# Gates of a mixture of experts: broadcast by TensorE against broadcast by DMA from a DRAM scratch

## The chip, the cores and the metric

One core of one Trainium2 chip runs the whole program. The metric is the device time of one execution in microseconds; lower is better. Below, batch b is one of four sequences (0 to 3) and a pair is one or two tiles of 128 hidden units of the experts.

## The reference, cut to what matters

The layer adds a selective scan over a context to `x`, and then a feed-forward layer of 2 shared and 32 routed experts, of which each token takes 6. All arrays are fp32: `x` is (4, 256, 256), the context (4, 256, 128), each expert's hidden size is 176.

```python
x = x + ssm(ctx, layernorm(x))              # scan over 256 steps, 256 channels x 16 states
xf = layernorm(x)                           # tokens x 256
shared = sum(relu(xf @ sw1[e] + sb1[e]) @ sw2[e] + sb2[e] for e in range(2)) / 2
logits = xf @ router_w + router_b
p, i = top_k(softmax(logits), 6); p = p / p.sum(-1)
gates = zeros(tokens, 32).at[rows, i].add(p)
routed = sum(gates[:, e:e+1] * (relu(xf @ rw1[e] + rb1[e]) @ rw2[e] + rb2[e]) for e in range(32))
out = x + shared + routed
```

## The kernel before

Everything lies transposed: features or hidden units on the 128 partitions, the 256 tokens of a batch on the free axis. The hidden units of all experts are laid end to end: 3 tiles of 128 for the shared ones, 44 for the routed ones (32 x 176 = 44 x 128, so most tiles hold units of two experts). They are worked in 24 pairs of tiles, `PAIRS`; pair 0 has the shared tiles 0 and 1, pair 1 only tile 2, and pairs 2 to 23 are routed.

A pair goes through the engines like this. TensorE makes the first layer into PSUM tile `z` with three fp32r products for each of two halves of the features (high and low parts of weights and input, L474 to L476), 12 matmuls. ScalarE adds the bias and takes the relu into `hg` (L613). TensorE has meanwhile made `gb`, the gates spread over the partitions: one matmul for each tile of a constant 0/1 matrix `selg` with `gst`, the 32 gates of the 256 tokens as three bf16 parts stacked on 96 partitions (L483). VectorE multiplies `hg` by `gb` (L796; pairs 0 and 1 are scaled by 1/2 at L798 instead). Three pairs later (`SKEW`) TensorE adds the second layer into `acc` (`second_layer`, L455): 4 fp32 matmuls, which the trace shows as 8 pieces, in batches 0 to 2, and 12 fp32r matmuls in the last batch, where ScalarE, GpSimd and VectorE make high and low parts (`split`). The trace calls `hg` by the tile it is a view of, `stage`, and drops digits from names, so `w` is `w2` or `w1` and `x` is `x1`.

Beside the pairs of batch b run the steps of the scan and router of the next batches, at pairs that tables name (`UNITS`, `ZGATE`, `BACK`, `NEXT`): in pairs 0 to 15 one unit of the scan each (`bu`, scan and product with C on VectorE, decay on ScalarE, the spread of B in even pairs and of C in odd ones on TensorE, L368 and L377, a fold on GpSimd), `stats` in pair 2, `zmul` in pair 10, and after pair 16 the norm, the router's logits and `gates`. The order on each engine is fixed by the program; engines wait for each other by semaphores. The run begins with a head (0 to 91 us) in which the first batch's scan has no expert work beside it. Batch 0 is opened by the lists in `OPEN`.

The gates of a batch are made in `gates` (L772) on VectorE, split into three bf16 parts (L786 to L789), turned by TensorE in pair 1 (`turn`, L429), and copied by ScalarE into `gst` and `gT` (L623, L624). `gT`, the fp32 form, is needed for the second layer's bias in pair 4. PSUM is full: `z` 2 banks, `gb` 2, `acc`, `bb`, `cc`, `misc` one each. So the first layer of pair p waits for the product of pair p - 2, the last reader's turn of both double buffers:

```python
if exists(b, p, 2):
    pe.wait_ge(S["hg_done"], b * NP + p - 1)
```

SyncE issues every DMA. In the expert phase that is one load of second-layer weights a pair, into a ring of six (`load_w2`), as soon as the second layer that frees the slot is done (`next_w2`), one store of the output and one load of the next `x1` a batch.

## Time and profile before

| what | value |
| --- | --- |
| time, median of 3 runs (range) | 433.68 us (433.26 to 436.71) |
| the profiled execution's own time | 433.63 us |
| its span, first to last instruction | 431.6 us |
| mean granted TensorE clock | 0.952 of full |
| busy: PE, DVE, ACT, POOL | 91%, 72%, 50%, 28% |
| the chain's share: PE, DVE, issue, ACT | 80%, 12%, 6%, 1% |
| DMA busy share, all of it in queue 1 (SyncE's) | 28.8% |

The chain is the sequence of work that ended last, followed back from the final instruction; an engine's share of it, and not its busy share, says how much of the time hangs on that engine. TensorE's rows overlap: one that is listed as 0.28 us long is followed by the next after 0.12, so differences between starts are what counts.

### The profile page before, as it was taken

How to read it: one execution, taken by the hardware profiler on the slowest of the kernel's cores; microseconds unless marked ns; L12 is line 12 of the kernel's file. 1: busy time of each engine (PE TensorE's matmuls, PEld its weight loads, DVE VectorE, ACT ScalarE, POOL GpSimd, SP SyncE). 2: the span in 40 equal slices, each digit the busy share in tenths (PEclk: the TensorE clock that was granted, in tenths of full speed). 3: DMA queues.
4: the chain of work that ended last, by engine and by line, in shares of the span. 5: the costliest groups of instructions: out<-in, count | busy, mean ns of one | idle time of the engine just before them, and what ended most of it. 6: DMA issues, size and time to landing. Idle time of an engine off the chain costs nothing.

```text
span 431.6 us, 7326 instructions
## 1 busy us (share of the span) xinstructions
PE 392.4 (91%) x2559; PEld 350.5 (81%) x2559; DVE 310.2 (72%) x544; ACT 215.9 (50%) x482; POOL 119.5 (28%) x88
## 2 busy tenths in 40 slices
PE   5565588589999999999999999999999999999996
PEld 3343366478899999978999989889999999999996
DVE  3499997799798767898898568898984544344443
ACT  3777625446443434565443436565432345556562
POOL 0654432013233200033333000233331023344432
PEclk8659889669999999999999999999999999999999
DMA  7344473002222322331222212332222224233320
GB/s 225 104 137 110 136 199 144 2 25 74 73 75 57 90 52 60 95 101 50 74 71 73 73 49 69 105 90 69 75 73 74 74 61 123 73 80 93 83 65 26
DMA packets 18879, 36.49 MB, mean 85 GB/s; under 512 B 2082, under 2 KB 4932, under 8 KB 18756
## 3 DMA queue, kind: packets, MB, share of 16 engines
q1 hardware_dynamic: 18852, 36.13, 28.8%
q8 instruction: 16, 0.26, 0.2%
q14 instruction: 11, 0.09, 0.1%
HBM read 35.08 MB, written 1.05 MB: 84 GB/s over the span
## 4 chain that ended last, share of the span: by engine, by line
PE 80%; DVE 12%; issue 6%; ACT 1%; DVEq 0%; ACTq 0%
PE acc L455 34%; PE z L474 10%; PE z L476 9%; PE z L475 9%; PE gb L483 4%; DVE bu L702 3%; PE z L387 2%; DVE bu L695 2%; PE acc L353 2%; PE bb L368 1%; PE cc L377 1%; PE acc L460 1%; PE bb L395 1%; PE misc L414 1%; PE cc L402 1%
## 5 line engine op out<-in xcount | busy, mean ns | idle before, releaser
L613 ACT ACTIVATE stage<-z,par 128x256 f32<-128x256 f32 x188 | 79.0, 471 | 159.6 <-PE z L476 159.5
L455 PE MATMUL acc<-stage,w 128*128 128x256 f32 x564 | 134.6, 381 | 0.0
L474 PE MATMUL z<-xh,w1l 128*128 128x256 f32 (+1 forms) x376 | 120.5, 321 | 0.0
L455 PEld LDWEIGHTS acc<-stage,w 128*128 128x128 f32 x564 | 102.6, 191 | 12.3
L796 DVE TENSOR_TENSOR stage<-stage,gb 128x512 f32<-128x512 f32 x88 | 60.3, 686 | 70.5 <-ACT stage L613 69.6
L846 POOL TENSOR_TENSOR ya<-ya,pr 128x512 f32<-128x512 f32 x42 | 54.8, 1305 | 196.7 <-DVE pr L713 196.7
L475 PE MATMUL z<-xl,w1h 128*128 128x256 f32 (+1 forms) x376 | 106.7, 284 | 0.0
L476 PE MATMUL z<-xh,w1h 128*128 128x256 f32 (+1 forms) x376 | 106.7, 284 | 0.0
L702 DVE TENSOR_TENSOR_SCAN bu<-dA,bu 128x512 f32<-128x512 f32 x64 | 78.6, 1237 | 2.0 <-ACT dA L566 0.4
L474 PEld LDWEIGHTS z<-xh,w1l 128*128 128x128 f32 x376 | 71.9, 191 | 4.0 <-issue 2.2
L475 PEld LDWEIGHTS z<-xl,w1h 128*128 128x128 f32 x376 | 72.1, 192 | 1.7
L476 PEld LDWEIGHTS z<-xh,w1h 128*128 128x128 f32 x376 | 72.0, 191 | 0.0
L566 ACT ACTIVATE dA<-delta,aneg 128x255 f32<-128x255 f32 x128 | 57.4, 502 | 16.3 <-DVE bu L702 15.5
L863 POOL TENSOR_TENSOR w2l<-w,w2h 128x512 fp32r<-128x512 f32 (+1 forms) x24 | 31.8, 1324 | 68.7 <-ACT w2h L620 68.7
L695 DVE TENSOR_TENSOR bu<-bb,du 128x512 f32<-128x512 f32 x64 | 43.1, 683 | 1.3 <-PE bb L368 1.3
L713 DVE TENSOR_TENSOR pr<-bu,cc 128x512 f32<-128x512 f32 x50 | 33.9, 685 | 12.2 <-PE cc L377 8.7
L830 POOL TENSOR_TENSOR w1l<-stage,w1h 128x1024 fp32r<-128x1024 f32 (+1 forms) x12 | 28.6, 2382 | 40.3 <-ACT w1h L511 23.6
L483 PE MATMUL gb<-gst,selg 96*128 96x256 bf16 x176 | 35.2, 282 | 0.0
L455 PE MATMUL acc<-hh,w2l 128*128 128x256 f32 x94 | 28.0, 298 | 0.0
L455 PE MATMUL acc<-hl,w2h 128*128 128x256 f32 x94 | 26.3, 280 | 0.0
L455 PE MATMUL acc<-hh,w2h 128*128 128x256 f32 x94 | 26.2, 279 | 0.0
L377 PE MATMUL cc<-bcs,selbc 96*128 96x256 bf16 x64 | 13.7, 300 | 11.3 <-DVE pr L713 7.8
(122 smaller groups left out, 408.2 us busy)
## 6 DMA issues: line engine op xcount, KB each, us to landing
w<-in_w SPq DMA_DIRECT2D x92, 256.0 KB, 2.7
stage<-in_w SPq DMA_DIRECT2D x11, 512.0 KB, 3.6
selg<-in_selg SPq DMA_DIRECT2D x1, 1056.0 KB, 7.7
x<-in_xT SPq DMA_DIRECT2D x4, 256.0 KB, 3.9
out<-x SPq DMA_DIRECT2D x4, 256.0 KB, 2.6
xr<-in_xr SPq DMA_DIRECT2D x1, 768.0 KB, 9.8
w<-in_w SPq DMA_DIRECT2D x4, 128.0 KB, 2.0
par<-in_par SPq DMA_DIRECT2D x1, 385.5 KB
```

The lines of the kernel that those rows point to most:

```text
L455: mm = pe.matmul(acc[:, k, :], weights, h, start=t + k + n == 0, stop=last, skip_group_check=True)
L474: pe.matmul(z[p % 2][:, i, :], w1l[:, t, one], xh_, start=k == 0, stop=False)
L475: pe.matmul(z[p % 2][:, i, :], w1h[:, t, one], xl_, start=False, stop=False)
L476: mm = pe.matmul(z[p % 2][:, i, :], w1h[:, t, one], xh_, start=False, stop=k == KD - 1)
L483: mm = pe.matmul(gb[p % 2][:, i, :], selg[:, t - NT_S, :], gst[:], start=True, stop=True)
L566: ins = act.activation(dA[:, k, j * L + 1:(j + 1) * L], delta[:, k, 1:L], ACT.Exp, scale=aneg[:, n:n + 1])
L613: ins = act.activation(hg[:, p % 4, i, :], z[p % 2][:, i, :], ACT.Relu, bias=b1[:, t:t + 1])
L695: dve.tensor_tensor(bu[:, k, :].rearrange("p (j l) -> p j l", j=2), bb[:], du[:, k:k + 1, :].broadcast_to([P, 2, L]), ALU.mult).then_inc(S ...
L702: dve.tensor_tensor_scan(bu[:, k, :], dA[:, k, :], bu[:, k, :], 0.0, ALU.mult, ALU.add).then_inc(S["scan_done"], 1)
L713: dve.tensor_tensor(products(b, c)[:, k, :], bu[:, k, :], cc[:].rearrange("p a b -> p (a b)"), ALU.mult).then_inc(S["prod_done"], 1)
L796: ins = dve.tensor_tensor(hg[:, p % 4], hg[:, p % 4], gb[p % 2][:], ALU.mult)
L846: pool.tensor_tensor(ya[:, k, :], ya[:, k, :], pr[:, k, :], ALU.add).then_inc(S["y_folded"], 1)
```

## The change

The gate no longer goes through TensorE. Four things change together.

1. The experts are tiled anew. The first 128 hidden units of each of the 32 experts make one tile each (pairs 2 to 17, `NSINGLE` = 16), so one gate holds for a whole tile; the remaining 48 units of each, end to end, make 12 tiles (pairs 18 to 23).
2. `gT` is stored to a DRAM scratch, `gates`, and read back with a partition step of 0: one DMA for each of the 16 single pairs (`gate_one`, 256 KB into the ring `gone` of four), and 40 DMAs of 16 to 48 rows for the remainder (`gate_rem`, 1.5 MB into `grem`), four in each of pairs 4 to 13. SyncE issues all of them, 57 more in a batch.
3. ScalarE writes the relu back into its PSUM bank, and VectorE makes the product from PSUM and the gate in SBUF into `hg`. `gb`'s two banks go to `z`, which has four, so the first layer of pair p waits for the product of pair p - 4.
4. The turn has no bf16 part, VectorE's bf16 split goes, and the turn moves from pair 1 to the end of pair 23 of the batch before (batch 0: pair 0), so that the gates leave early.

To make room, `xr` and `ctxT` are kept for two batches and loaded as the run goes, and `hh` and `hl` have three buffers in place of four.

```diff
@@ tables and buffers
-TURN_AT = 1
+ZB = 4
+GRING = 4
...
-        ("xh", 21), ("xl", 21), ("top", 21), ("ex", 22), ("gates", 22)]
+        ("xh", 21), ("xl", 21), ("top", 21), ("ex", 22), ("gates", 22), ("turn", 23)]
...
-BEHIND = ("mean", "logits", "xall", "dt")
+BEHIND = ("mean", "logits", "xall", "dt", "turn")
...
-OPEN = [[("gates", 0)],
+OPEN = [[("gates", 0), ("turn", 0)],
...
-        z = [ps(f"z{i}", [P, 2, L]) for i in range(2)]
-        gb = [ps(f"gb{i}", [P, 2, L]) for i in range(2)]
+        z = [ps(f"z{i}", [P, 2, L]) for i in range(ZB)]
@@ SyncE
+            def gate_one(b, p):
+                e = 2 * (p - SINGLE0)
+                eng.dma_start(gone[:, p % GRING], gates_d[b % 2, e:e + 2, :].rearrange("(o e) l -> o e l", o=1).broadcast_to(
+                    [P, 2, L])).then_inc(ld_g[p % GRING], 16)
+
+            def gate_rem(b, part):
+                for e, t, at, n in SEGMENTS[part::REMPARTS]:
+                    eng.dma_start(grem[at:at + n, t, :], gates_d[b % 2, e:e + 1, :].broadcast_to([n, L])).then_inc(ld_rem, 16)
...
+            for b in range(B):
+                eng.wait_ge(S["gates_done"], b + 1)
+                eng.dma_start(gates_d[b % 2], gT[0:NR, :]).then_inc(S["spilled"], 16)
+                if b:
+                    eng.wait_ge(S["hg_done"], b * NP)
+                eng.wait_ge(S["spilled"], 16 * b + 16)
+                for p in range(SINGLE0, SINGLE0 + GRING):
+                    gate_one(b, p)
                 for p in range(NP):
...
+                    if SINGLE0 <= p < SINGLE0 + NSINGLE - GRING:
+                        eng.wait_ge(S["hg_done"], b * NP + p + 1)
+                        gate_one(b, p + GRING)
+                    if 4 <= p < 4 + REMPARTS:
+                        gate_rem(b, p - 4)
...
+                    if p >= SKEW:
+                        if b < B - 1 or p - SKEW < NP - RING:
+                            next_w2(b, p - SKEW)
+                    elif b:
+                        next_w2(b - 1, p - SKEW + NP)
@@ TensorE
+                elif name == "turn":
+                    pe.wait_ge(S["g34_done"], b + 1)
+                    for t in range(2):
+                        mm = pe.matmul(misc[0:NR + NSH, 1, t * P:(t + 1) * P], g34[:, t, :], ident, start=True, stop=True)
+                    mm.then_inc(S["turned"], 1)
...
-                if exists(b, p, 2):
-                    pe.wait_ge(S["hg_done"], b * NP + p - 1)
+                if exists(b, p, ZB):
+                    pe.wait_ge(S["hg_done"], b * NP + p - ZB + 1)
...
-                if PAIRS[p][0] >= NT_S:
-                    if PAIRS[p][0] == NT_S:
-                        pe.wait_ge(ld_selg, 16)
-                        pe.wait_ge(S["gates_done"], b + 1)
-                    for i, t in enumerate(PAIRS[p]):
-                        mm = pe.matmul(gb[p % 2][:, i, :], selg[:, t - NT_S, :], gst[:], start=True, stop=True)
-                    mm.then_inc(S["gb_ready"], 1)
-                if p == TURN_AT:
-                    turn(b)
@@ ScalarE
-                    ins = act.activation(hg[:, p % 4, i, :], z[p % 2][:, i, :], ACT.Relu, bias=b1[:, t:t + 1])
+                    ins = act.activation(z[p % ZB][:, i, :], z[p % ZB][:, i, :], ACT.Relu, bias=b1[:, t:t + 1])
...
-                if p == TURN_AT:
-                    act.wait_ge(S["turned"], b + 1)
-                    act.activation(gst[:], miscb[0:3 * NR, 0:L], ACT.Copy)
-                    act.activation(gT[:], misc[0:NR + NSH, 1, :], ACT.Copy).then_inc(S["gates_done"], 1)
@@ VectorE
-                    own.then(dve.tensor_copy(g3[:, :, 0, :], g34[:, :, 0:NR]))
-                    own.then(dve.tensor_tensor(gr[:], g34[:, :, 0:NR], g3[:, :, 0, :], ALU.subtract))
-                    own.then(dve.tensor_copy(g3[:, :, 1, :], gr[:]))
-                    dve.tensor_tensor(g3[:, :, 2, :], gr[:], g3[:, :, 1, :], ALU.subtract).then_inc(S["g3_done"], 1)
...
-                if PAIRS[p][0] >= NT_S:
-                    dve.wait_ge(S["gb_ready"], b * NPR + p - (NP - NPR) + 1)
-                    ins = dve.tensor_tensor(hg[:, p % 4], hg[:, p % 4], gb[p % 2][:], ALU.mult)
+                if p >= SINGLE0 + NSINGLE:
+                    r = 2 * (p - SINGLE0 - NSINGLE)
+                    dve.wait_ge(ld_rem, (b + 1) * 16 * len(SEGMENTS))
+                    ins = dve.tensor_tensor(hg[:, p % 4], z[p % ZB][:], grem[:, r:r + 2, :], ALU.mult)
+                elif p >= SINGLE0:
+                    dve.wait_ge(ld_g[p % GRING], b * (16 * NSINGLE // GRING) + 16 * ((p - SINGLE0) // GRING + 1))
+                    ins = dve.tensor_tensor(hg[:, p % 4], z[p % ZB][:], gone[:, p % GRING], ALU.mult)
```

TensorE, an even pair of the loop's body. Before:

```order
L476 MATMUL z<-xh,w1h 128x256
L483 MATMUL gb<-gst,selg 128x256 x2
L361 ISA
L368 MATMUL bb<-bcs,selbc 128x256 [waits bu_done]
L368 MATMUL bb<-bcs,selbc 128x256
L455 MATMUL acc<-stage,w 128x256 [waits ld_w2_3,hg_done]
L455 MATMUL acc<-stage,w 128x256 x3
```

After:

```order
L512 MATMUL z<-xh,w1h 128x256
L399 ISA
L406 MATMUL bb<-bcs,selbc 128x256 [waits bu_done]
L406 MATMUL bb<-bcs,selbc 128x256
L477 REGISTER_ALU
L491 MATMUL acc<-stage,w 128x256 [waits ld_w2_3,hg_done]
L491 MATMUL acc<-stage,w 128x256 x3
```

The two `gb` matmuls between the first layer and the scan's B are gone; the rest keeps its place, and what the first layer waits for is two pairs older.

TensorE at the turn of the gates. Before, it stands between the first layer of pair 1 and its second layer:

```order
L476 MATMUL z<-xh,w1h 128x256
L432 MATMUL misc<-identb,g 96x128 [waits g3_done]
L432 MATMUL misc<-identb,g 96x128
L434 MATMUL misc<-par,g 34x128 x2
L377 MATMUL cc<-bcs,selbc 128x256 x2
L442 REGISTER_ALU
L455 MATMUL acc<-stage,w 128x256 [waits ld_w2_4,hg_done]
L455 MATMUL acc<-stage,w 128x256 x3
```

After, it stands behind the second layer of pair 23, ahead of the next batch's first layer:

```order
L491 MATMUL acc<-stage,w 128x256 [waits ld_w2_2,hg_done]
L491 MATMUL acc<-stage,w 128x256 x3
L462 MATMUL misc<-par,g 34x128 [waits g34_done]
L462 MATMUL misc<-par,g 34x128
L503 ISA [waits xl_done]
L510 REGISTER_ALU [waits w1l_done,hg_done]
L510 MATMUL z<-xh,w1l 128x256
```

The wait for VectorE's gates has moved some two pairs ahead, and the bf16 transposes through `identb` are gone.

SyncE at the start of batch 1. Before, it has nothing between the weight loads but the output's store:

```order
L308 DMA w<-in_w 128x512 [waits l2_done] x19
L308 DMA w<-in_w 128x256 [waits l2_done]
L308 DMA w<-in_w 128x512 [waits l2_done] x4
L316 DMA out<-x 256x1x256 [waits ot_done]
L329 UNCONDITIONAL_BRANCH
L329 ISA
L308 DMA w<-in_w 128x512 [waits l2_done]
```

After:

```order
L318 DMA w<-in_w 128x256 [waits l2_done]
L318 DMA w<-in_w 128x512 [waits l2_done]
L346 DMA gates<-gT 32x256 [waits gates_done]
L336 DMA gone<-gates 128x512 [waits spilled,hg_done]
L336 DMA gone<-gates 128x512 x3
L318 DMA w<-in_w 128x512 [waits l2_done] x2
L336 DMA gone<-gates 128x512 [waits hg_done]
L318 DMA w<-in_w 128x512 [waits l2_done]
L336 DMA gone<-gates 128x512 [waits hg_done]
L328 DMA out<-x 256x1x256 [waits ot_done]
L318 DMA w<-in_w 128x512 [waits l2_done]
```

The store of the gates and four gate loads stand ahead of the weight loads for the last three second layers of the batch before, and a weight load now stands behind a wait for VectorE's product of the same pair.

## Rows read from the trace of the kernel before

**Rows 1.** The page, part 4: the chain's share by engine and line.
```profile
PE acc L455 34%; PE z L474 10%; PE z L476 9%; PE z L475 9%; PE gb L483 4%; DVE bu L702 3%; PE z L387 2%; DVE bu L695 2%; PE acc L353 2%; PE bb L368 1%; PE cc L377 1%; PE acc L460 1%; PE bb L395 1%; PE misc L414 1%; PE cc L402 1%
```

**Rows 2.** The chain in order of time: start us, us, what.
```profile
181.29 0.69 DVE bu L695
...
193.69 1.73 PE acc L455 x8
...
209.37 1.73 PE acc L455 x8
212.98 1.73 PE acc L455 x8
...
413.12 1.41 PE acc L455 x12
416.18 1.40 PE acc L455 x12
```

**Rows 3.** TensorE's timeline, pair 23 of batch 2 and pair 0 of batch 3.
```profile
345.90 0.47 PE L474 MATMUL z<-xh,w1l 128*128 128x256 f32 x1
...
347.52 0.39 PE L483 MATMUL gb<-gst,selg 96*128 96x256 bf16 x2
347.75 1.89 PE L455 MATMUL acc<-stage,w 128*128 128x256 f32 x8
349.29 0.47 PE L474 MATMUL z<-xh,w1l 128*128 128x256 f32 x1
...
352.44 0.47 PE L474 MATMUL z<-xh,w1l 128*128 128x256 f32 x1
```

**Rows 4.** Timeline of batch 1, pairs 8 to 14: TensorE's row, then VectorE's [idle].
```profile
201.54 0.40 PE L483 MATMUL gb<-gst,selg 96*128 96x256 bf16 x2
...
202.70 0.69 DVE L796 TENSOR_TENSOR stage<-stage,gb 128x512 f32<-128x512 f32 x1 [0.76 <-ACT stage L613]
...
205.98 0.69 DVE L713 TENSOR_TENSOR pr<-bu,cc 128x512 f32<-128x512 f32 x1 [0.73 <-PE cc L377]
...
213.19 0.69 DVE L713 TENSOR_TENSOR pr<-bu,cc 128x512 f32<-128x512 f32 x1 [0.68 <-PE cc L377]
213.80 0.68 DVE L731 TENSOR_TENSOR sz<-sz,cv 128x512 f32<-128x512 f32 x1
...
224.34 0.69 DVE L796 TENSOR_TENSOR stage<-stage,gb 128x512 f32<-128x512 f32 x1
```

**Rows 5.** Timelines at the start of batch 0 and around that of batch 1.
```profile
79.46 0.39 DVE L784 TENSOR_SCALAR g<-em,rsm 128x32 f32<-128x32 f32 x2
...
80.60 0.22 DVE L789 TENSOR_TENSOR g<-gr,g 128x64 bf16<-128x64 f32 x1
...
86.13 0.69 DVE L796 TENSOR_TENSOR stage<-stage,gb 128x512 f32<-128x512 f32 x1 [0.78 <-ACT stage L613]
...
168.37 0.39 DVE L784 TENSOR_SCALAR g<-em,rsm 128x32 f32<-128x32 f32 x2
...
168.66 1.89 PE L455 MATMUL acc<-stage,w 128*128 128x256 f32 x8
...
179.35 0.69 DVE L796 TENSOR_TENSOR stage<-stage,gb 128x512 f32<-128x512 f32 x1 [0.54 <-ACT stage L613]
```

**Rows 6.** Transfers: L324, issues by size, then queue 1 in 188.7 to 192.3 and 203 to 206.6.
```profile
L324 SPq DMA_DIRECT2D x<-in_xT x2: 628/639/650, 188.8 to 279.6; - x2
...
DMA to landing us min/median/max: 3.2/3.4/3.6
...
w<-in_w SPq DMA_DIRECT2D x4, 128.0 KB, 2.0
...
selbc<-in_selbc SPq DMA_DIRECT2D x1, 6.0 KB, 4.7
...
q1 hardware_dynamic: 416, 0.52, 48.0%
...
q1 hardware_dynamic: 144, 0.26, 25.8%
```

More of the change, by code:

```diff
@@ L26 @@
 NC = NS // 2
+NSINGLE = NR // 2
+REM = HID - P
+NREM = NR * REM // P
 NBC = 3 * 2 * NS
@@ L50 @@
 B2_AT = 4
+SINGLE0 = NP - NPR
+REMPARTS = 10
 UNITS = []
@@ L65 @@
         ("dtl", 21), ("split", 21), ("dt", 21), ("sp", 22), ("delta", 23)]
-BEHIND = ("mean", "logits", "xall", "dt")
+BEHIND = ("mean", "logits", "xall", "dt", "turn")
+SEGMENTS = []
+for _e in range(NR):
+    _at = _e * REM
+    while _at < (_e + 1) * REM:
+        _to = min((_e + 1) * REM, (_at // P + 1) * P)
+        SEGMENTS.append((_e, _at // P, _at % P, _to - _at))
+        _at = _to
 HEAD = [(("warm", None, 11), 0), ("xin", 0), ("cv0", 0), ("taps", 0), (("warm", "conv_done", 6), 0), ("econv", 0), ("uclip", 0),
@@ L320, in next_w2 @@
                 load_w2((p + RING) % NP)
-            def next_x(b):
-                eng.wait_ge(S["stored"], 16 * b + 16)
-                eng.dma_start(x1[:, (b + 1) % 2], xT_d[:, :, b + 1, :]).then_inc(ld_xT, 16)
-            for p in range(NP):
-                next_w2(0, p)
-            store(0)
-            with eng.Fori(1, B - 1) as i:
-                for p in range(NP):
-                    if p == 2:
-                        next_x(i)
-                    next_w2(i, p)
-                store(i)
@@ L335, in _ @@
-            for p in range(NP - RING):
-                next_w2(B - 1, p)
+            def gate_one(b, p):
[5 more added lines that the diff above has]
+                    eng.dma_start(grem[at:at + n, t, :], gates_d[b % 2, e:e + 1, :].broadcast_to([n, L])).then_inc(ld_rem, 16)
@@ L716, in step @@
                     zs.start(b)
-                    dve.wait_ge(ld_xr, 16 if first(b) else 32)
+                    dve.wait_ge(ld_xr, 16 * (b + 1))
                     for k in range(KD):
-                        zs.did(dve.bn_stats(st6[:, k, :], xr[:, b, k, :]))
+                        zs.did(dve.bn_stats(st6[:, k, :], xr[:, b % 2, k, :]))
                     zs.wait()
@@ L931 @@
         "in_w2": w2,
-        "in_selg": selg.reshape(3 * NR, NT_R, P),
         "in_selbc": selbc,
@@ L938 @@
     out = nc.dram_tensor("out_0", (P, KD, B, L), F32, kind="ExternalOutput").ap()
-    xattn_ffn_kernel(nc, *args, out)
+    gates = nc.dram_tensor("gates", (2, NR, L), F32).ap()
+    xattn_ffn_kernel(nc, *args, gates, out)
     r = run_bass_kernel_spmd(nc, [arrays], core_ids=[0])
```

100 lines of the change are left out of this document (54 added, 46 removed).

## The prediction

> **What bounds the kernel now.** I read the chain of waits first, by line: the product of gates on TensorE (`gb`, L483) holds 4% of it, and the two expert layers (L455, L474 to L476) hold 62% [rows 1]. That alone would say "remove 4%". The chain in order of time says where the 4% counts. From 91 us on it is `acc` matmuls at a fixed spacing, one second layer for each pair of expert tiles: 3.61 us in the pairs that share TensorE with the scan's B and C (209.37 to 212.98) and 3.06 us in the last batch (413.12 to 416.18). The exception is a stretch at the start of each of the first three batches, where VectorE's `bu` and scan hold it: in batch 1 from 181.29, in the middle of pair 2, until TensorE takes the chain back at 193.69, in pair 6 [rows 2]. So a microsecond taken off TensorE is a microsecond off the time in pairs 7 to 23 of batches 0, 1 and 2 and in all of batch 3, and nothing in pairs 3 to 6 of the first three.
>
> **What one gate product costs.** Pair 23 of batch 2 has it, pair 0 of batch 3 hasn't, and neither has anything else beside its 12 `z` and 8 `acc` pieces: from first `z` to first `z` 349.29 - 345.90 = 3.39 us against 352.44 - 349.29 = 3.15. Inside the pair, `gb` starts at 347.52 and `acc` at 347.75 [rows 3]. Both views give 0.23 to 0.24 us for two matmuls of 256 columns; I take 0.235. There are 22 such pairs in a batch.
>
> **The change part by part, against the profiled execution's 433.63 us (0.05 us below the median shown).**
>
> The gate products go. In batches 0, 1 and 2 the pairs 7 to 23 count, 17 x 0.235 = 4.0 us each. In batches 1 and 2 pair 2 counts as well, since the residual's last sum, which opens VectorE's stretch, waits for the second layer behind that pair's `gb`: 0.235. In batch 3 all 22 count: 5.2.
>
> The turn loses its two bf16 transposes, and the fp32 ones stay: about half of a `gb`, 0.11 us in each of batches 1 to 3 (an estimate from the column count, 256 against 512, and the 0.235). It moves from pair 1 to behind the second layer of pair 23. TensorE then waits there for the gates on VectorE: they are ready at 168.37 + 0.39 = 168.8, and the second layer that starts at 168.66 runs 1.89 us, to 170.5 [rows 5], so the wait is covered by 1.7 us. ScalarE waits longer in pair 23, ahead of the next pair's relu, but that relu's `z` isn't written before the turn either.
>
> ScalarE's relu now writes PSUM, and VectorE's product reads `z` from PSUM and the gate from SBUF in place of the other way round. The trace has no ScalarE write to PSUM, so it is bounded from both sides: VectorE waits 0.76 us for the relu at pair 8 and not at all at pair 14 [rows 4], so a tenth either way on each of the pair's two relus costs or gives nothing. The product keeps its shape and its one PSUM operand, so I leave it at 0.69 us [rows 4]; TensorE comes to need it four pairs later and not two, which only loosens things. The shared experts' scaling now reads PSUM; it can't cost more than the product's 0.69 for the same 512 columns, and falls where VectorE waits anyway.
>
> Does VectorE keep up when TensorE's pair shrinks to 3.61 - 0.235 = 3.375 us? From the product of pair 8 to that of pair 14 it takes 224.34 - 202.70 = 21.64 us, of which 0.73 and 0.68 are idle: 20.23 of work, with `zmul`'s 0.68 in it [rows 4]. TensorE's six pairs come to 6 x 3.375 = 20.25. The two are level. What saves TensorE from waiting is that its B matmuls need only the previous pair's `bu`. From the end of `z` to the start of the product are 202.70 - 201.54 = 1.16 us, and product and `bu` take twice 0.69 more, so VectorE could fall behind by 3.375 - 1.16 - 1.38 = 0.84 us before TensorE waits, and `zmul` puts it 0.68 behind. So I count nothing, but with a margin of 0.15 us.
>
> The gates now travel. In batch 1: written 168.8, turn behind the layer at 170.5, copy by ScalarE, 171.2; the store to the scratch; then the first load of a pair's gates. For the store the nearest rows are 2.0 us (128 KB, quiet queue) and 4.7 (6 KB, at the crowded start); the queue is quiet here, so 2.3. For the load the nearest is `x`, also 256 KB in rows of 1 KB: 3.4 us [rows 6]. It lands at 176.9, or at 179.3 with the 4.7. Pair 2's product wants it at 179.35 - 0.23 = 179.1 [rows 5]: 2.2 us to spare, or 0.2 too few. Batches 2 and 3 are alike. Batch 0 has no second half of pair 23 to hide in. The four VectorE steps of the bf16 split go (80.60 + 0.22 against 79.85), but the shared scaling is slower; gates at 80.1, `gT` some 0.9 us later, plus 5.7: 86.7, where the product of pair 2 stood at 86.13 [rows 5]. VectorE paces there, so I count 0.5 us lost (0 to 3).
>
> SyncE: each pair from 4 to 13 now issues one gate load, four remainder loads and one `w2` load. Priced at the 0.64 us that the `x` load's issue takes [rows 6], all six need 3.84 us of a pair's 3.375, an upper end, since the remainder's have at most 48 rows each and not 256. The deficit of 0.47 a pair comes to 4.7 us after ten, less than the three pairs (10 us) by which `w2` and gates are ahead. The scratch store also holds back three `w2` loads at each batch's start by some 3 us, inside the same 10. The transfers: `x` and `w2` together took 48.0% of 16 engines for 3.6 us = 27.6 engine-us, `w2` alone 25.8% = 14.9 [rows 6], so 256 KB in 1 KB rows cost 12.8. A pair from 4 to 13 needs 14.9 + 12.8 + 0.6 x 12.8 = 35.4 of the 16 x 3.375 = 54. It fits, if reading one row of the scratch 128 times costs what reading 128 rows does, which no row shows.
>
> The sum: 4.0 - 0.5, twice 4.0 + 0.235 + 0.11, and 5.2 + 0.11: 3.5 + 8.7 + 5.3 = **17.5 us**, 433.6 to **416 us**.
>
> The Trainium skill speaks against part of this. Its page "DMA: Bandwidth & Descriptors", section "Anatomy of one DMA", fits 2.0 us plus bytes over 436 GB/s to each DMA of GpSimd's path. By that, the 40 remainder loads of a batch would come to 84 us if none overlapped, as long as a batch. The trace disagrees on the overlap: `x` and `w2` both landed inside 3.6 us. For the store and the first load the page gives 4.7 us together, against my 5.7, which would free batch 0 of its 0.5.
>
> **The rivals.**
>
> VectorE paces pairs 8 to 15 too. For it: the two engines are level there, with 0.15 us in hand behind `zmul`. Against it: VectorE's two idle waits of 0.73 and 0.68 in those pairs [rows 4], which shrink before TensorE loses anything. Then only pairs 16 to 23 pay in three batches, 24 x 0.235 = 5.6, and batch 3's 5.3, and the small terms 0.2: 11 us, **422 us**.
>
> The gates come late. If store and load take 8 to 10 us together, batch 0 loses 2.5 to 4.5 and batches 1 and 2 up to 2 each (batch 3 has no scans, and its second layer comes three pairs later): **421 to 425 us**. For it: a round trip through DRAM that the trace doesn't hold. Against: 2.2 us to spare by the quiet rows.
>
> The gates' transfers become the bound, and the kernel is **slower**. Place: pairs 4 to 13. Let a 1 KB gate packet cost k times an `x` packet, since all 16 engines read the same row. Ten pairs need 149 + 205k engine-us, and 16 x (33.8 + 10) = 700 are there before anything waits: k = 2.7. The whole gain is gone at k = 3.0 (4.4 us a batch more); at k = 4 a batch loses 16.8 us and the time is 416 + 67 = **483 us**. For it: a same-row read isn't in the trace. Against: a third of the engines' time is free, and k must be three.
>
> The gap isn't given back: the next matmuls wait out what `gb` filled, or a new wait of the same size comes in. **431 to 434 us**. Against: pair 0 of batch 3 lacks `gb`, and is shorter by just that [rows 3].
>
> More than forecast: VectorE's stretches shrink as well, and every product counts: 88 x 0.235 + 0.4 = 21.1, **412.5 us**. Nothing takes work out of those stretches.
>
> **How the numbers follow.** Forecast 0.57 (its own range 414 to 418.5), VectorE 0.17, late gates 0.11, transfers 0.06, nothing given back 0.05, more 0.04. The range takes in the first three and the last: 412 to 425. A change within 1% (429.3 to 438.0) is about what a measurement here can't tell from none. Faster by over 1% is forecast, VectorE, late gates and more: 0.89. Within 1%: 0.05. Slower: 0.06.
>
> **What the changed profile would show.** Chain spacing in the last batch 2.82 us, in pairs 9 to 13 of batches 0 to 2 3.38 (3.61 there: the VectorE rival, with TensorE's B matmuls waiting for `bu`). No wait of VectorE's product for a gate load but in pair 2 of batch 0. VectorE's stretch at a batch's start as long as before, some 12 us. DMA share near 0.65 in pairs 4 to 13; at 0.95 and more the transfers' rival stands. It would be wrong if the granted clock fell in the emptier TensorE queue, or if the product or the relu changed its duration by over a tenth.

## The result and the profile after

The changed kernel takes **419.93 us** (median of 4 runs, 418.02 to 421.79), against 433.53 for the kernel before beside it: a ratio of **0.967, with a 95% interval of 0.960 to 0.974**. The profiled execution took 418.02 us with a span of 416.2, so against the 433.63 of before it gained 15.6 us where the prediction's sum said 17.5. The median lies 1.9 us above the profiled run because two of the four runs took 421.4 and 421.8 us, for which there is no trace.

The page's chain by line comes first, as in [rows 1]: the product of gates has left it, the two expert layers hold 62% as before, and VectorE's `bu` and scan (L721, L728) 8% for 5%.

```profile
PE acc L491 34%; PE z L510 10%; PE z L511 9%; PE z L512 9%; DVE bu L728 5%; DVE bu L721 3%; PE z L425 2%; PE acc L391 2%; PE bb L406 1%; PE cc L415 1%; PE acc L496 1%; DVE stage L822 1%; PE misc L452 1%; PE cc L440 1%; PE bb L433 1%
```

The chain in order of time (start us, us, what), at the places of [rows 2]:

```profile
177.67 0.69 DVE bu L721
...
190.07 1.77 PE acc L491 x8
...
204.93 1.73 PE acc L491 x8
208.33 1.73 PE acc L491 x8
...
252.72 1.73 PE acc L491 x8
254.44 0.56 PE misc L462 x4
...
256.86 1.73 PE acc L491 x8
...
398.42 1.41 PE acc L491 x12
401.24 1.41 PE acc L491 x12
```

Read it against [rows 2] as distances between equal points. The spacing in pairs 9 to 13 is 208.33 - 204.93 = 3.40 us for 3.61, in the last batch 401.24 - 398.42 = 2.82 for 3.06: each of the pairs gives back 0.21 to 0.24 us. VectorE's `bu` in pair 2 of batch 1 starts at 177.67 for 181.29, and TensorE takes the chain back at 190.07 for 193.69: 3.62 us ahead at both, so that nothing is won or lost inside that stretch. Near the end the lead is 416.18 - 401.24 = 14.9 us.

The turn is the odd piece. Four pieces of `misc` (L462) hold 0.56 us of the chain, and the second layers on its two sides are 256.86 - 252.72 = 4.14 us apart where a pair with as much scan work and no turn takes 3.40.

VectorE's timeline in pairs 8 to 11 of batch 1, the place of [rows 4] (start us, us, engine, line, what, and in brackets its idle time before):

```profile
198.79 0.69 DVE L822 TENSOR_TENSOR stage<-z,gone 128x512 f32<-128x512 f32 x1 [0.45 <-ACT z L643]
...
202.36 0.68 DVE L822 TENSOR_TENSOR stage<-z,gone 128x512 f32<-128x512 f32 x1
...
205.69 0.68 DVE L822 TENSOR_TENSOR stage<-z,gone 128x512 f32<-128x512 f32 x1
...
208.54 0.69 DVE L739 TENSOR_TENSOR pr<-bu,cc 128x512 f32<-128x512 f32 x1 [0.25 <-PE cc L415]
209.15 0.68 DVE L757 TENSOR_TENSOR sz<-sz,cv 128x512 f32<-128x512 f32 x1
```

Its idle waits of 0.76 and 0.68 us in [rows 4] are now 0.45 and 0.25. Without a wait it needs 205.69 - 202.36 = 3.33 us a pair, and TensorE 3.40: it keeps up, by 0.07 us a pair.

The transfers: queue 1 of the whole run, and the issues by size with the time to landing.

```profile
q1 hardware_dynamic: 37428, 58.27, 46.6%
...
w<-in_w SPq DMA_DIRECT2D x92, 256.0 KB, 3.3
gone<-gates SPq DMA_DIRECT2D x64, 256.0 KB, 3.8
```

A gate load lands in 3.8 us, near the 3.4 taken for it, and the weight load that shares the queue in 3.3, where the kernel before had 2.7. No wait of VectorE for a gate load is in the trace. In batch 0 the first gated product is late all the same, and the timeline there says by what (the last three fields of TensorE's first row are its wait for the gates):

```profile
79.99 1.07 PE L462 MATMUL misc<-par,g 128*34 128x128 f32 x4 [4.41 <-DVE g L810]
80.99 0.58 PE L510 MATMUL z<-xh,w1l 128*128 128x256 f32 x1
...
82.99 1.74 SPq L336 DMA_DIRECT2D gone<-gates  x4
...
86.17 0.81 ACT L643 ACTIVATE z<-z,par 128x256 f32<-128x256 f32 x2 [1.38 <-PE z L512]
87.02 0.69 DVE L822 TENSOR_TENSOR stage<-z,gone 128x512 f32<-128x512 f32 x1 [0.73 <-ACT z L643]
```

TensorE stands 4.41 us waiting for the gates with the whole first layer of pair 1 queued behind the turn, then does turn and layers mostly at the 1.2 GHz level (granted clock 0.55 from 80 to 87 us; a `z` matmul takes 0.41 us there and 0.28 elsewhere). The product waits for ScalarE's relu, which waits for TensorE, not for the load: 87.02 against the 86.13 of [rows 5].

### The profile page after: what moved, and what is told of

Its sections match the earlier page's. It is cut to its first block, busy times and chain, and to the rows that moved or that the text cites. A ratio compares the mean times of both kernels' runs of the same rounds, so it can differ in the third digit from the quotient of the medians.

```text
span 416.2 us, 7115 instructions
## 1 busy us (share of the span) xinstructions
PE 374.5 (90%) x2383; PEld 334.5 (80%) x2383; DVE 307.5 (74%) x527; ACT 214.8 (52%) x478; POOL 119.2 (29%) x88
## 2 busy tenths in 40 slices
DMA packets 37456, 58.62 MB, mean 141 GB/s; under 512 B 5778, under 2 KB 15284, under 8 KB 37428
## 3 DMA queue, kind: packets, MB, share of 16 engines
q1 hardware_dynamic: 37428, 58.27, 46.6%
## 4 chain that ended last, share of the span: by engine, by line
PE 76%; DVE 15%; issue 6%; ACT 1%; DVEq 1%; ACTq 0%
PE acc L491 34%; PE z L510 10%; PE z L511 9%; PE z L512 9%; DVE bu L728 5%; DVE bu L721 3%; PE z L425 2%; PE acc L391 2%; PE bb L406 1%; PE cc L415 1%; PE acc L496 1%; DVE stage L822 1%; PE misc L452 1%; PE cc L440 1%; PE bb L433 1%
## 5 line engine op out<-in xcount | busy, mean ns | idle before, releaser
L643 ACT ACTIVATE z<-z,par 128x256 f32<-128x256 f32 x188 | 76.3, 443 | 137.3 <-PE z L512 137.3
L491 PEld LDWEIGHTS acc<-stage,w 128*128 128x128 f32 x564 | 102.8, 191 | 12.2
L728 DVE TENSOR_TENSOR_SCAN bu<-dA,bu 128x512 f32<-128x512 f32 x64 | 78.7, 1240 | 1.7
L822 DVE TENSOR_TENSOR stage<-z,gone 128x512 f32<-128x512 f32 x64 | 43.9, 686 | 31.0 <-ACT z L643 30.5
L890 POOL TENSOR_TENSOR w2l<-w,w2h 128x512 fp32r<-128x512 f32 (+1 forms) x24 | 31.3, 1306 | 62.8 <-ACT w2h L650 62.8
L721 DVE TENSOR_TENSOR bu<-bb,du 128x512 f32<-128x512 f32 x64 | 42.9, 679 | 0.0
L819 DVE TENSOR_TENSOR stage<-z,grem 128x512 f32<-128x512 f32 x24 | 16.6, 690 | 31.5 <-ACT z L643 31.5
L491 PE MATMUL acc<-hh,w2h 128*128 128x256 f32 x94 | 26.3, 280 | 0.0
L491 PE MATMUL acc<-hh,w2l 128*128 128x256 f32 x94 | 26.3, 280 | 0.0
L491 PE MATMUL acc<-hl,w2h 128*128 128x256 f32 x94 | 26.3, 280 | 0.0
```

Of the source, the lines that this page charges most:

```text
L491: mm = pe.matmul(acc[:, k, :], weights, h, start=t + k + n == 0, stop=last, skip_group_check=True)
L643: ins = act.activation(z[p % ZB][:, i, :], z[p % ZB][:, i, :], ACT.Relu, bias=b1[:, t:t + 1])
L721: dve.tensor_tensor(bu[:, k, :].rearrange("p (j l) -> p j l", j=2), bb[:], du[:, k:k + 1, :].broadcast_to([P, 2, L]), ALU.mult).then_inc(S ...
L728: dve.tensor_tensor_scan(bu[:, k, :], dA[:, k, :], bu[:, k, :], 0.0, ALU.mult, ALU.add).then_inc(S["scan_done"], 1)
L822: ins = dve.tensor_tensor(hg[:, p % 4], z[p % ZB][:], gone[:, p % GRING], ALU.mult)
L890: pool.tensor_tensor(w2l[:, p % 4, 0:n, :], w2[:, p % RING, 0:n, :], w2h[:, p % 4, 0:n, :].bitcast(F32), ALU.subtract).then_inc(S["w2l_don ...
```

## The experiments

In brackets behind a median stand its range, the ratio to the kernel before as measured beside it, and that ratio's interval. The kernel before had a median of 436.33 us beside experiments 5, 6, 8 and 11 and of 433.25 to 433.96 beside the others, so from one experiment to the next compare times and not ratios. Runs of one kernel spread by 3 us or so (see the last section), so where a profiled run is compared I also give D, the time from the start of VectorE's last gate step in batch 0 (`g<-em`, 79.55 us in the changed kernel) to the start of the last 12-piece second layer (404.07): **324.5 us** in the changed kernel. D leaves out the head, where most of the spread arises, but not the clock behind it: from the gates step to the bias layer in pair 7 (L496) it takes 27.9 us in the changed kernel and 26.8 in experiment 3, which is the same program up to there, with granted clocks of 0.55 and 0.76 from 80 to 87 us. So a difference of D under 1 us shows nothing, and where it matters I count from that bias layer (107.49 us) on.

**1. The turn by two transposes.** A 32-column bf16 matmul takes the wait.

```diff
+                    pe.matmul(misc[:, 1, 0:32], ones[:, 0:P], ones[:, 0:32], start=True, stop=True)
                     for t in range(2):
-                        mm = pe.matmul(misc[...], g34[:, t, :], ident, start=True, stop=True)
+                        mm = pe.transpose(misc[...], g34[:, t, :], ident)
```

> The changed kernel with the gates turned by PE transposes, as before the change, in place of fp32 matmuls; a 32-column bf16 matmul in front carries the wait. In the changed kernel the turn is four pieces in 0.56 us of the chain, and the second layers around it are 4.14 us apart in place of 3.39. Theory A (the fp32 matmul form costs double): two pieces fewer, about 0.2 us at each of three turns, 0.4 to 0.7 in all, and 0.4 at batch 0's turn with its clock at half, all together 0.8 to 1.1 us less. Theory B (what costs is the wait and the restart around the turn, whatever its form): less than 0.3 us.

Measured: **415.88 us** (415.34 to 419.55; ratio 0.960, 0.957 to 0.963), profiled 415.96, D 322.1. Its chain around the turn of batch 1:

```profile
251.74 1.73 PE acc L492 x8
...
253.48 0.23 PE misc L463 x2
...
255.36 1.73 PE acc L492 x8
```

Two pieces of 0.23 in all for four of 0.56, and 3.62 us over the turn for 4.14: 0.33 of the 0.52 lies in the pieces and 0.19 between them and the next second layer. The other two turns gave 0.52 and 0.51, so the three come to 1.6 us, more than the 0.4 to 0.7 that I expected of them. The rest of D's 2.4 lies in batch 0 ahead of its bias layer, where the granted clock differs too (0.74 for 0.55), so it isn't shown to be the turn's. The form of the turn, which I had costed as a gain of 0.1 us a batch, was worth 0.5 us a batch on the wrong side. In batch 0 the gated product now does wait for the load: the chain has the store, then the gate load, and the product at 86.46. The two take 1.48 + 3.44 = 4.9 us, where the prediction priced 5.7 and named 4.7 as the other figure.

```profile
81.44 1.48 DMA gates<-gT
...
82.93 3.44 DMA gone<-gates
```

**2 and 3. Padding TensorE.** Four matmuls of 256 bf16 columns (0.46 us) ahead of the first layer, in pairs 3 to 6 of batches 0 to 2 in one kernel, in pairs 9 to 12 in the other.

```diff
+                if 9 <= p <= 12 and not (type(b) is int and b == B - 1):
+                    for _ in range(4):
+                        pe.matmul(z[p % ZB][:, 0, :], ones[:, 0:P], ones[:], start=True, stop=True)
```

> The changed kernel with four more bf16 matmuls of 256 columns, 0.46 us, ahead of the first layer in pairs 3 to 6 of batches 0 to 2. Theory A (VectorE paces the start of a batch, so TensorE work there is free): 0 to 1 us more; pairs 3 and 4 have 1.4 us of wait to fill and take 0.92, pairs 5 and 6 have 0.67 and take 0.92. Theory B (TensorE paces everywhere): 12 x 0.46 = 5.5 us more.

> The same four matmuls in pairs 9 to 12 of batches 0 to 2. Theory A (TensorE paces pairs 7 to 23): 5.5 us more, 0.46 for each of 12 pairs. Rival (VectorE paces pairs 8 to 15 once the gate product is gone): under 2 us more, since 0.2 us a pair would already be covered.

Measured: pairs 3 to 6 **418.98 us** (418.49 to 422.46; 0.968, 0.964 to 0.971), profiled 418.90, D 325.6, so +1.1 for 5.5 us of added work. Pairs 9 to 12 **425.25 us** (423.54 to 427.12; 0.981, 0.977 to 0.984), profiled 423.54, D 328.7, +4.1, the profiled time +5.5; from the bias layer of batch 0 on it is +5.3. The chain of the second:

```profile
203.99 1.73 PE acc L491 x8
207.82 1.73 PE acc L491 x8
211.64 1.73 PE acc L491 x8
```

3.82 and 3.83 us a pair for 3.40: what is added to TensorE there is paid nearly in full, and beside VectorE's stretch four fifths of it are free. That is the map on which the prediction counted its pairs.

**4. Every gate load of 12 pairs doubled**, as two more 128 KB copies into three slots.

```diff
+                for r in range(2):
...
+                    if dumped[j]:
+                        eng.wait_ge(ld_d[j], 16 * dumped[j])
+                    dumped[j] += 1
+                    eng.dma_start(dump[:, j], gates_d[b % 2, e + r:e + r + 1, :].broadcast_to([P, L])).then_inc(ld_d[j], 16)
```

> The changed kernel with each gate load of pairs 6 to 17 issued a second time into an unused buffer that nothing waits for but its own reuse. Theory A (the transfers are hidden; a third of the DMA engines' time is free in pairs 4 to 13): DMA share near 0.9 there in place of 0.69, landings later by a microsecond or two, time within 1 us. Rival (the transfers are at their limit and set part of the time): 3 us more or over, with VectorE's product or TensorE's second layer waiting for a DMA.

Measured: **436.01 us** (433.98 to 439.54; 1.006, 1.002 to 1.011), profiled 433.98, D 339.1: **+14.6 to 16 us** where I expected one at most. My margin for the transfers (a gate packet may cost 2.7 times an `x` packet) was not a margin for this. Its queue 1 holds 55.9% of the engines' time; SyncE's own timeline showed more:

```profile
297.73 0.42 SPq L320 DMA_DIRECT2D w<-in_w  x1
298.20 0.43 SPq L350 DMA_DIRECT2D gone<-gates  x1
298.67 1.25 SPq L346 DMA_DIRECT2D dump<-gates  x2
299.97 1.83 SPq L355 DMA_DIRECT2D grem<-gates  x4
301.85 0.42 SPq L320 DMA_DIRECT2D w<-in_w  x1
```

One issue follows the other without a gap, 4.12 us from one weight load to the next. Three theories were left: the bytes, SyncE's series of issues, the slots' waits (15.2 us in the trace). Experiments 9 and 10 tell them apart.

**5. No gate copies after batch 0.** In batch 0 too, only the first four single copies and the remainder's are left; the expectation says neither this nor the right counts, which are 16 copies and 40 part copies a batch. VectorE's waits for the missing loads are left out with them.

```diff
                 for p in range(SINGLE0, SINGLE0 + GRING):
-                    gate_one(b, p)
+                    if not b:
+                        gate_one(b, p)
...
-                        gate_one(b, p + GRING)
-                    if 4 <= p < 4 + REMPARTS:
+                    if 4 <= p < 4 + REMPARTS and not b:
```

> The changed kernel, with the gate rows copied out of the scratch in batch 0 alone: in batches 1 to 3 the 22 copies and 20 part copies a batch are left out, and the products there use the gates of batch 0 that still lie in SBUF, so the output isn't the reference's in those batches. Store of the gates, weights, order of TensorE and VectorE are unchanged. Theory A (TensorE alone sets batches 1 to 3 of the changed kernel; the copies lie beside it): nothing to win, 417.5 to 419 us, profiled span within 1 us of 416.2, and a spacing of 3.39 us in the pairs 9 to 13 as now. Rival (doubling the copies of 12 pairs a batch cost 16 us, so the single ones cost something too, through the weight loads queued with them): up to two thirds of that in three batches, 406 to 414 us, and the spacing in the pairs 9 to 13 falls below 3.3 us. What both expect: the landing time of a weight copy falls from 3.3 us towards the 2.0 us of the kernel before.

Measured: **418.36 us** (417.0 to 419.36; 0.960, 0.955 to 0.965), profiled 419.36, D 324.2, the changed kernel's less 0.3. Queue 1 falls to 31.3% and the weight load's landing to 2.7 us, the figure of the kernel before (the 2.0 expected is that of its 128 KB loads), and nothing is won: in the changed kernel the copies are hidden.

**6. The relu back in SBUF**, the product from SBUF and SBUF.

```diff
-ins = act.activation(z[p % ZB][:, i, :], z[p % ZB][:, i, :], ACT.Relu, bias=b1[:, t:t + 1])
+ins = act.activation(hg[:, p % 4, i, :], z[p % ZB][:, i, :], ACT.Relu, bias=b1[:, t:t + 1])
...
-ins = dve.tensor_tensor(hg[:, p % 4], z[p % ZB][:], gone[:, p % GRING], ALU.mult)
+ins = dve.tensor_tensor(hg[:, p % 4], hg[:, p % 4], gone[:, p % GRING], ALU.mult)
```

(the same for the remainder's product and the shared experts' scaling)

> The changed kernel with the second half of its title undone: the relu goes from the PSUM bank to SBUF, and the gate product is made from SBUF and SBUF into SBUF, everything else as it is. Theory A (TensorE sets the time, the place of the relu does nothing for it): 417.5 to 420 us; the relu back from 442 to some 470 ns a tile, the product between 680 and 700 ns. Rival B (the product from PSUM is what lets VectorE keep up in the pairs 8 to 14; from SBUF it is over 100 ns dearer or delayed by GpSimd, 7 pairs in 4 batches): 421 to 424 us with waits of TensorE for it. Rival C (reading PSUM is what the product pays for): from SBUF it takes under 600 ns, and the time falls by no more than 2 us, since VectorE sets only the first pairs of a batch.

Measured: **427.17 us** (426.52 to 427.69; 0.981, 0.976 to 0.987), profiled 426.75, D 333.1: **+8.5 us** by D, 7.2 by the medians. None of my three theories had that much; B named GpSimd, but at 421 to 424 us. The median of the product's own time didn't move (686 ns for 684). What moved stands in the timeline beside it, here of VectorE and GpSimd:

```profile
198.21 0.68 DVE L822 TENSOR_TENSOR stage<-stage,gone 128x512 f32<-128x512 f32 x1
...
198.47 1.57 POOL L873 TENSOR_TENSOR ya<-ya,pr 128x512 f32<-128x512 f32 x1 [2.05 <-DVE pr L739]
...
199.53 1.59 DVE L728 TENSOR_TENSOR_SCAN bu<-dA,bu 128x512 f32<-128x512 f32 x1
...
201.82 0.68 DVE L822 TENSOR_TENSOR stage<-stage,gone 128x512 f32<-128x512 f32 x1
```

and in the changed kernel:

```profile
202.62 1.28 POOL L873 TENSOR_TENSOR ya<-ya,pr 128x512 f32<-128x512 f32 x1 [2.85 <-DVE pr L739]
...
203.68 1.30 DVE L728 TENSOR_TENSOR_SCAN bu<-dA,bu 128x512 f32<-128x512 f32 x1
```

GpSimd's fold is released by VectorE's product of `bu` and `cc` and starts while the gate product runs. With both operands of that in SBUF the fold takes 1.57 us and not 1.28, so it ends later and reaches into the scan, which takes 1.59 and not 1.23 to 1.30. VectorE comes to 201.82 - 198.21 = 3.61 us a pair, over TensorE's 3.40, and holds the chain. The Trainium skill has this as a rule ("SBUF — State Buffer", section "Who interferes with whom"): a VectorE instruction with two SBUF inputs contends with a GpSimd instruction that reads SBUF, and one with at most one SBUF input, outside the two-port performance modes, doesn't. The two timelines agree, with 0.3 us for each of the two delayed instructions.

Which of the two pays depends on who is first. In pair 11 `zmul` (L757) stands ahead of the product, the fold is 0.34 us ahead of it, and it is the product that takes 1.77 us:

```profile
212.96 1.57 POOL L873 TENSOR_TENSOR ya<-ya,pr 128x512 f32<-128x512 f32 x1 [2.05 <-DVE pr L739]
213.30 1.77 DVE L822 TENSOR_TENSOR stage<-stage,gone 128x512 f32<-128x512 f32 x1
```

Seven of the 64 products take 0.87 to 1.77 us, and their mean goes from 686 to 753 ns; in the changed kernel none takes over 0.69.

**7. The same with GpSimd's fold on 8 columns in place of 512**, to take the collision away and nothing else.

```diff
-pool.tensor_tensor(ya[:, k, :], ya[:, k, :], pr[:, k, :], ALU.add)
+pool.tensor_tensor(ya[:, k, 0:8], ya[:, k, 0:8], pr[:, k, 0:8], ALU.add)
```

> The kernel of the run e6_relu_sbuf (relu to SBUF, product from SBUF and SBUF, 427.2 us), in which GpSimd's fold of the products (ya plus pr, 42 of 128x512) works on 8 columns instead of 512, so that GpSimd is all but idle beside VectorE; the output isn't the reference's, since the rest of the scan's output is left unsummed. Theory C (e6 lost its time to a collision of two engines: GpSimd's fold takes 1.58 us there where it took 1.28, and the scan beside it 1.59 where it took 1.23 to 1.30, so that VectorE needs 3.62 us a pair, more than TensorE's 3.39): the scan is back at 1.22 to 1.30 us, a pair at 3.39, and the time at 417 to 420 us. Rival (a product from SBUF makes VectorE late by itself): the scan or the product stays dearer and the time at 424 to 428 us.

Measured: **417.94 us** (416.89 to 421.56; 0.964, 0.956 to 0.972), D 324.2. The whole 8.5 us is back, with the product still from SBUF. What this kernel leaves out is most of the fold.

```profile
203.82 1.22 DVE L728 TENSOR_TENSOR_SCAN bu<-dA,bu 128x512 f32<-128x512 f32 x1
```

The scans are back at 1.22 us and the products at a mean of 0.69. So the collision of GpSimd's fold with VectorE is shown as the cause; how the 8.5 us split between scans and products isn't.

**8. Two `z` banks in place of four** (`ZB = 2`).

> The changed kernel with two z banks in the place of four (the two that the gate product's banks gave back stand empty), so that the first layer of a pair waits for the product of the second last pair. Theory A (the product ends some 1.5 us after its first layer, and 3 us before the bank is wanted again): 417.5 to 420 us, no wait of TensorE for the product over 0.5 us. Rival (the four banks carry part of the gain, because VectorE's stretch of 12 us at the start of a batch delays the products there, and TensorE now has to wait at the banks): 422 to 430 us, with waits of TensorE at its first layers in the pairs 2 to 7.

Measured: **419.79 us** (418.2 to 421.75; 0.963, 0.957 to 0.969), profiled 421.75, D 323.6; TensorE has no wait for the product in the list of waits. The two banks that the gate products gave back are worth nothing that these runs can show.

**9 and 10. What doubling cost.** Two more issues a pair with a quarter of the bytes, and 12 slots; and one more issue a pair of 128 KB, into 3 slots.

```diff
+                    eng.dma_start(dump[:, j], gates_d[b % 2, e + r:e + r + 1, 0:64].broadcast_to([P, 64])).then_inc(ld_d[j], 16)
...
+                eng.dma_start(dump[:, j], gates_d[b % 2, e:e + 1, :].broadcast_to([P, L])).then_inc(ld_d[j], 16)
```

> The changed kernel with two more loads in each of the 12 pairs in which the gates_x2 run had them, issued in the same place by the same queue, but a quarter as long (128 rows of 256 B each instead of 1 KB) and into 12 slots, so that SyncE never waits for a slot. Theory S (what cost 16 us there is SyncE's time in series: in the pairs 4 to 13 its trace shows 0.42 for the weight load, 0.43 for the gate load, 1.25 for the two more, 1.83 for the four part copies, with the gaps some 4.1 us a pair, over TensorE's 3.39): two issues of 0.42 us leave 3.7 to 3.9 us a pair, still over 3.39, so 424 to 431 us, and SyncE busy without a gap over the pairs 4 to 13. Theory T (the bytes of the transfers cost it, 46% becoming 56% of the engines): these bring a quarter of those bytes, 418 to 421 us.

> The changed kernel with one more 128 KB load (1 KB rows) a pair in the same 12 pairs, half of the gates_x2 run in bytes and in issues, into 3 slots, so that its slot is always free. Theory S (SyncE's series): 0.42 + 0.43 + 0.42 + 1.83 and four gaps of 0.05 make 3.3 us a pair, just under TensorE's 3.39, so 418 to 421 us. Theory T (bytes): half of what the double ones cost, 424 to 428 us.

Measured: two small ones **428.02 us** (425.11 to 431.45; 0.988, 0.981 to 0.994), profiled 428.49, D 334.8, +10.3. One of 128 KB **419.89 us** (419.36 to 421.33; 0.970, 0.968 to 0.972), D 325.3, +0.7, and +1.6 from the bias layer of batch 0 on, all of it in batch 3. Queue 1 is at 47.3% in the dear one and at 55.9% in the cheap one, which ends the theory of the bytes; neither has a wait for a slot. The number of packets does go with the time (51,252, 44,340, and 37,428 in the changed kernel), but in the last batch the weight loads land in 4.2 us in the dear one and 4.5 in the cheap one: what comes late there is their issue. SyncE's timeline in the last batch, of the run with two small ones, then of the changed kernel:

```profile
371.67 0.42 SPq L320 DMA_DIRECT2D w<-in_w  x1
372.13 0.43 SPq L350 DMA_DIRECT2D gone<-gates  x1
372.61 0.91 SPq L346 DMA_DIRECT2D dump<-gates  x2
373.55 1.82 SPq L355 DMA_DIRECT2D grem<-gates  x4
375.42 0.42 SPq L320 DMA_DIRECT2D w<-in_w  x1
```

```profile
369.59 0.42 SPq L318 DMA_DIRECT2D w<-in_w  x1
370.06 0.43 SPq L336 DMA_DIRECT2D gone<-gates  x1
370.53 1.82 SPq L341 DMA_DIRECT2D grem<-gates  x4
372.40 0.42 SPq L318 DMA_DIRECT2D w<-in_w  x1
```

One behind the other, an issue takes SyncE 0.47 us from start to start, whatever it carries. Eight of them are 3.75 us a pair, six are 2.81, and TensorE's pair is 2.82 in the last batch. Up to the last batch the run with two small ones keeps pace with the changed kernel (its first 12-piece second layer starts at 350.12 us, the changed kernel's at 349.81); it ends 10.5 us behind, all but 0.3 of it in batch 3, with ScalarE waiting 21.1 us for weight loads. SyncE in series, not the transfers, is the next limit on this kernel, and **in the last batch the changed kernel stands exactly on it**, with hardly a gap between issues and only the lead of the earlier loads to spare (ScalarE waited 1.0 us for weights there). That lead takes up one more issue a pair, which has ScalarE wait 10.7 us for weights and costs 1.6, but not two. The four part copies of the remainder are 1.87 of the 2.81. Experiment 4 lost 12.2 us in batch 3 and 2.4 elsewhere; that its waits for slots made it the dearer of the two wasn't tried apart.

**11. The turn in pair 1 in batch 0**, on top of experiment 1.

```diff
-OPEN = [[("gates", 0), ("turn", 0)],
-        [(n, 1) for n in (("B", 0), ...
+OPEN = [[("gates", 0)],
+        [("turn", 0)] + [(n, 1) for n in (("B", 0), ...
```

> The changed kernel with the turn of the gates by two transposes instead of two fp32 products (as in the run e1_transpose, 415.9 us), and in batch 0 alone the turn stands one pair later, behind the first layer of pair 1, so that this doesn't wait for it. Theory A (in batch 0 the first layer of pair 1, 6 matmuls at half clock, stood behind the turn and so reached the relu of pair 2 late; the gates' load isn't what is late): hg(2) 0.5 to 1 us earlier than in e1_transpose where it waited, 415.0 to 415.9 us. Rival (the gates' load is what the product of pair 2 waits for, store 3.4 us behind a later turn): the first gated product waits for a transfer and starts later than 87.1 us, 416 to 417.5 us.

Measured: **416.18 us** (415.05 to 419.66; 0.958, 0.953 to 0.963), profiled 416.11, D 321.4, 0.7 below experiment 1. The product of pair 2 waits 1.81 us for its load and starts at 86.72, the load having landed at 86.62; with the gates themselves 0.8 us later in this run, that is 6.0 us behind the gates, against 6.6 in experiment 1. Between the two I can't tell a difference in the medians.

**12. TensorE kept busy before batch 0's turn**, 36 matmuls of ones, on top of experiment 1.

```diff
+                    if first(b):
+                        for _ in range(36):
+                            pe.matmul(z[3][:, 0, :], ones[:, 0:P], ones[:], start=True, stop=True)
```

> The kernel of the run e1_transpose (the turn by two transposes, 415.9 us) with 36 matmuls of bf16 ones into an idle z bank in front of batch 0's wait for the gates, while TensorE would wait, so that its clock, which fell to the 1.2 GHz level at 80 us in every run so far, is at 2.4 when the turn comes. Theory A (in batch 0 the first gated product waits for the gates' load, and from there to 98.5 us VectorE is what is late, so TensorE's clock there is worth nothing): 415 to 416.5 us. Rival (TensorE at 1.2 GHz from 80 to 94 us holds batch 0 back): the first layers of pairs 1 to 4 finish earlier and the end comes 1 to 3 us earlier, 413 to 415 us. Rival B (the added matmuls run over the time at which the gates are ready): 416.5 to 418 us.

Measured: **416.34 us** (415.69 to 416.46; 0.961, 0.959 to 0.962), profiled 415.69, D 321.6. The windows around it, 80 to 87 us, this run's row and then that of experiment 1 (busy time by engine, granted clock, DMA share, GB/s):

```profile
80.00:87.00 7.00, 3.13 (x27) 2.71 (x25) 4.25 (x9) 4.05 (x10) 0.00 (x0) 1.00 0.38 132
```

```profile
80.00:87.00 7.00, 4.40 (x25) 3.86 (x25) 3.77 (x7) 4.07 (x10) 0.00 (x0) 0.74 0.44 126
```

The granted clock is 1.00, the 2.4 GHz level, and TensorE is done 1.3 us sooner, but the load lands 3.14 us after its issue all the same. By D it gives 0.5 us, all of it ahead of the bias layer of pair 7, which neither the spread of D nor the medians can show.

## Why the prediction was right, and where not

**The forecast's mechanism holds, and one term is mis-sized.** 416.0 was said with 412 to 425 around it; it is 419.9, and the profiled run 418.0. The median lies outside the forecast's own 414 to 418.5; the traces account for the profiled run's 2.0 us, and the other 1.9 are in the spread of the runs. At 421 to 425 us the rivals of VectorE and of the late gates would have had times near the slower runs', but the trace has neither: no spacing of 3.61 us in pairs 9 to 13, and no product that waits for a gate load.

- *What one gate product costs*: 0.235 us said, 0.21 to 0.24 measured at both spacings. In the last batch the lead grows from 360.61 - 349.81 = 10.8 us at the first 12-piece layer to 15.4 at the end, 4.6, where the 20 products behind that layer were priced at 4.7.
- *Which pairs count*: experiments 2 and 3 paid 1.1 and 5.3 of 5.5 us in the places that were called free and paced. Only in batch 0 was the map off. The chain of the kernel before, at the gate products of that batch's pairs 3 and 4:

```profile
90.71 0.45 PE gb L483 x2
...
95.68 0.24 PE gb L483 x2
```

TensorE, not VectorE, holds it there from 87.48 us on, at first at the 1.2 GHz level. So the gate products of pairs 3 to 6, 0.45 and three of 0.24, could be won too. They made good the 0.9 us by which the first gated product is late: the bias layer in pair 7 starts 0.34 us earlier (107.49 for 107.83), where the sum had it 0.27 later.
- *The step that failed*, the term that is mis-sized, is "the turn loses its two bf16 transposes, and the fp32 ones stay", -0.11 us a batch. The fp32 transposes don't stay: the diff has `pe.matmul(...)` there where before had `pe.transpose(...)`, and the trace makes four pieces, 0.56 us in the chain, of two products with the identity. In batch 1 the lead falls from 7.29 us (252.72, before the turn) to 6.54 behind it, and regains 0.3 where the old turn stood: a cost of **0.43 us a batch** in place of a gain of 0.11, 1.6 us over three. Experiment 1 took that much back by restoring the transposes. With the two smaller corrections, 0.6 more in batch 0 as above and 0.22 for 0.235 us on each of 75 products (from 107.49 to the turn of batch 0 the lead grows by 3.51 us in 16 pairs), the sum is 17.5 - 1.6 + 0.6 - 1.1 = 15.4 us, against the 15.6 measured. That is closer than batch 0's opening allows, which by its clock differs by 1 us between runs; the turn's 1.6 is the part that an experiment shows.
- *Batch 0's late gates*: the time was near (86.7 said; 86.5 in experiment 1, where the load is what is waited for, and 87.0 in the changed kernel), the cause in the changed kernel wasn't. What is queued behind a wait counts: pair 1's first layer, which the kernel before has ahead of the same wait of 4.4 us, stands behind it now. The rival of late gates was priced too high besides: by its own terms 8 to 10 us make 418 to 424, and not 421 to 425.
- *VectorE keeps up*: right, by 0.07 us a pair, and for a reason that the prediction didn't hold. It left the product "at 0.69" because it keeps one PSUM operand; its duration indeed doesn't depend on that, but GpSimd's fold and the scan behind it do. With the gates in SBUF and the relu left there too, the rival "VectorE paces pairs 8 to 15" comes true, at 427 us (experiment 6) where I had priced it at 422. The relu's way into PSUM keeps 8.5 us of the gain.
- *SyncE*: the issue was priced at 0.64 us and the pair at 3.375. It is 0.47, and the pair that matters is the last batch's 2.82, which the prediction didn't put beside it. There it comes out level, and the lead that was taken for 10 us gives less: one more issue a pair, 4.1 us later for SyncE at the end of its series (389.02 for 384.90), costs 1.6 us, and two more, 10.2 later, cost 10.
- *The transfers' rival*: k = 2.7 was the wrong quantity. Doubled gate loads do cost 15 us, but through SyncE; with one more load a pair (experiment 10) the queue's share goes from 46.6% to 55.9% for 1.6 us. And a gate load isn't 256 packets of 1 KB: the 60 that experiment 5 leaves out are 7,680 packets of 2 KB, 128 each. An estimate from the queue's shares there: (46.6% of 416.2 us - 31.3% of 417.6) x 16 engines over the 20.5 MB left out make 13.0 engine-us for 256 KB, against the 12.8 taken for `x`, so k is near 1. The added 1 KB packets of experiments 4 and 10 come out dearer by the same reckoning, 15.9 and 26.3, on a fuller queue. DMA share in pairs 4 to 13 was said near 0.65; 0.69 in the window 277 to 300 us.

```profile
277.00:300.00 23.00, 22.96 (x144) 20.57 (x145) 21.12 (x27) 12.48 (x31) 8.15 (x7) 1.00 0.69 207
```

The fastest kernel of the study is the changed one with its turn by transposes, 415.9 us, with experiments 11 and 12, built on it, not to be told from it. Not settled is how much of SyncE's rare long issues (up to 3.7 us for four where 1.8 is usual) the last batch can take in other runs.

## What to carry to other kernels

When work moves from an engine to DMAs, add up the issuing engine's time too, all its issues of a loop step one behind the other, and set it against the shortest step of the loop, not the typical one. When an operand moves from PSUM to SBUF, look at what GpSimd does beside VectorE: most of the moved instructions may keep their time while their neighbours pay. And price a moved operation by the line in the diff, with what stands behind its wait on the same engine.

## What the runs showed of the hardware

- With issues one behind the other SyncE needs 0.47 us for each, for 32 KB as for 256 KB (0.42 to 0.43 in the row, the rest a gap), with an occasional one of 1 to 2 us more; one that stood behind a wait has 0.32 to 0.34 in the row.
- A relu of 128x256 into its own PSUM bank takes 442 ns (median of 188), into SBUF 469. The Trainium skill states that ScalarE writes to PSUM faster than to SBUF ("ScalarE: Activation LUTs", section "Step-by-step: what each stage is for"); the two medians agree.
- A two-SBUF-operand VectorE product delays a GpSimd add beside it from 1.28 to 1.57 us, and that the next scan from 1.23 to 1.59, where the product starts first; where the add starts first, the product takes 1.77 us for 0.69.
- Copying two gate rows of 1 KB each from the scratch to all 128 partitions lands in 3.8 us, the weight load of as many bytes from distinct rows beside it in 3.3.
- Turning two 128x34 fp32 tiles by two matmuls with the identity holds 0.56 us of the chain in four pieces, by two transposes 0.23 in two.
- Runs of one kernel spread over 3 us, and the two profiled runs that were the slowest of their four (experiments 5 and 8) were late in the head: in experiment 5 by 1.6 us at the last gate step of batch 0, and with two `z` banks that step starts at 84.11 us and not at 79.55, with TensorE at 0.50 granted clock and busy 8.00 of the 8 us from 72 to 80, where the changed kernel had 0.97 and 3.59; from there on both take the same time within 0.9 us.
